# A decoder layer with routed experts: three shared-expert groups ahead of the routed blocks instead of four, and a new order around them

## What is computed

```
logits = xt @ gate_w.T + gate_b;  w, idx = top_k(sigmoid(logits), 2);  w = w / (sum(w) + 1e-08)
for e in range(6):
    h = silu(xt @ ew1[e].T) * (xt @ ew3[e].T);  y = y + ge[:, e:e+1] * (h @ ew2[e].T)
z = silu(xt @ fc1.T) * (xt @ fc2.T) @ fc3.T
out = x + y + z
```

## Time and profile before

| what | us |
|---|---|
| median of three runs | 1301.81 |
| lowest and highest run | 1296.87 and 1304.25 |
| the profiled execution's own time | 1303.18 |
| its span, first to last instruction | 1301.4 |
| its mean granted TensorE clock | 0.975 of 2.4 GHz |

### The profile page before, as it was taken

How to read it: one execution, slowest core, us unless ns; L and a number is a source line. 1 busy time by engine, 2 the same in 40 slices (tenths; PEclk the granted TensorE clock), 3 DMA queues, 4 the chain that set the end, 5 groups by cost and what they waited for, 6 DMA issues and landing times.

```text
span 1301.4 us, 34483 instructions
## 1 busy us (share of the span) xinstructions
PE 1210.7 (93%) x10882; PEld 1099.3 (84%) x10882; DVE 874.3 (67%) x2904; ACT 765.7 (59%) x1800; POOL 505.5 (39%) x709
## 2 busy tenths in 40 slices
PE   4899999999999779999999999999999888999984
PEld 4799899899998667989999999999998777888884
DVE  3765654755655557778778878888777675555548
ACT  3454443443544327788888888888887654555530
POOL 2341332431414342254444444444444531333335
PEclk9999999999999899999999999999999988999996
DMA  9499900000000335655566666655565243333359
GB/s 209 104 223 231 208 0 0 0 0 0 0 0 23 87 95 127 154 151 148 142 152 145 153 154 153 153 149 146 143 168 142 71 122 96 98 106 99 108 143 249
DMA packets 131263, 151.39 MB, mean 116 GB/s; under 512 B 41107, under 2 KB 111108, under 8 KB 131156
## 3 DMA queue, kind: packets, MB, share of 16 engines
q1 hardware_dynamic: 124436, 134.55, 42.5%
q0 software_dynamic: 6160, 15.69, 3.7%
q10 hardware_dynamic: 576, 0.07, 0.1%
HBM read 79.27 MB, written 45.82 MB: 96 GB/s over the span
## 4 chain that ended last, share of the span: by engine, by line
PE 51%; DVE 4%; issue 2%; POOL 2%; DMA 2%; ACT 1%; SPq 1%; DVEq 0%; POOLq 0%; ACTq 0%
PE psum L884 9%; PE psum L1135 7%; PE psum L1158 6%; PE psum L1172 6%; PE psum L1307 6%; PE psum L1327 3%; PE psum L1104 2%; PE psum L1153 2%; PE psum L1200 2%; PE psum L1186 1%; PE psum L1219 1%; DVE x_res L2356 1%; PE psum L1298 1%; PE psum L1315 1%; DVE x_res L2350 1%
## 5 line engine op out<-in xcount | busy, mean ns | idle before, releaser
L2219 DVE CUSTOM_DVE_ANT_0 junk<-psum,biasq 112x375 f32<-112x375 f32 x512 | 267.1, 542 | 95.0 <-issue 62.7
L1677 ACT ACTIVATE pr<-psum 125x448 f32<-125x448 f32 x384 | 204.3, 541 | 40.7 <-PE psum L1158 36.7
L1158 PE MATMUL psum<-qst,kst 97*125 97x224 f32 x768 | 192.8, 316 | 5.1 <-ACT psum L1686 5.0
L1135 PE MATMUL psum<-kst,qst 96*112 96x376 f32 x512 | 170.2, 356 | 4.0 <-DVE smax L2219 3.4
L1158 PEld LDWEIGHTS psum<-qst,kst 97*125 97x125 f32 x768 | 138.0, 189 | 17.6 <-ACT psum L1686 11.9
L1686 ACT ACTIVATE psum<-flagk 125x448 f32<-125x448 bf16 x240 | 131.7, 549 | 6.5 <-ACT pr L1677 0.4
L725 POOL TENSOR_TENSOR rs<-rs,neg_half 112x1 f32<-112x1 f32 x32 | 18.3, 571 | 243.3 <-DVE rs L2132 243.3
L850 POOL DMA_INDIRECT routed_y<-yb,yrow x61 | 58.9, 966 | 123.8 <-ACT yb L1868 118.1
L1135 PEld LDWEIGHTS psum<-kst,qst 96*112 96x112 f32 x512 | 89.6, 180 | 15.8 <-DVE smax L2219 5.9
L1172 PE MATMUL psum<-pr,vaug 125*32 125x112 f32 x3072 | 94.8, 264 | 0.0
L767 POOL DMA_INDIRECT routed_h<-h,slot x64 | 76.8, 1199 | 29.1 <-PE psum L1158 16.2
(11 more groups left out here) (321 smaller groups left out, 3501.8 us busy)
## 6 DMA issues: line engine op xcount, KB each, us to landing
kst<-khi SPq DMA_DIRECT2D x64, 376.0 KB, 4.9
routed_h<-in_route_pad SPq DMA_DIRECT2D x6, 3640.0 KB
kst<-klo SPq DMA_DIRECT2D x32, 376.0 KB, 6.3
ctxT<-in_ctxT SPq DMA_DIRECT2D x32, 375.0 KB
hblk<-routed_h SPq DMA_DIRECT2D x61, 130.0 KB
qst<-qhi SPq DMA_DIRECT2D x128, 56.0 KB, 2.5
stage<-in_e SPq DMA_DIRECT2D x21, 256.0 KB, 3.4
maskq<-in_mask SPq DMA_DIRECT2D x32, 164.1 KB
```

Source lines behind the costliest of these rows:

```text
L1135: pe.matmul(bank[max_bank(n, par, hd)][0:T, 0:S2E], head(qst[par][0:ROWS], hd), pair(kst[par][0:ROWS], hd // 2), start=True, stop=True).th ...
L1158: mm = pe.matmul(bank[q % 2][0:KP, cols(i, 2 * T)], pair(kst[par], n)[:, cols(q // HPB, KP)], both(qst[par], n), start=False, stop=True, s ...
L1677: nc.scalar.activation(pr[q % PROBS][:].rearrange("k i q -> k (i q)"), bank[q % 2][0:KP, 0:GT], ACT.Exp, scale=1.0 / HD ** 0.5).then_inc(s ...
L2219: nc.vector.tensor_tensor_reduce(out=junk[:, hd % 2, :], in0=bank[max_bank(n, par, hd)][0:T, 0:S2], in1=biasq[:, par, :], scale=1.0, scala ...
```

## The change

`FRONT` is 3: group 3 moves from the front to the tail. SyncE loads three groups between blocks 3 and 4 (4, 6 and 7, the latter two into buffers of their own, `h3last[0]` and `h3last[1]`) and group 5 behind the last block. The products have six buffers instead of four. In the front, VectorE does the slots of row 31 and `plan_blocks` earlier, and eight of the twelve low parts of weights instead of twelve; GpSimd does the last four, after its last scatter. GpSimd also issues the scatter of row 30 before it decides row 31.

```diff
-FRONT = 4
+FRONT = 3
+PRODUCTS = 6
+TURNED = (0, 1, 2, 3, 4, 6, 7, 5)
...
+        def raw_shared(g):
+
+            return h3last[g - (G - 2)][:] if g >= G - 2 else h3lo[g % 2][:].bitcast(F32)
+
+        def turned_at(g):
+
+            return 16 * DC * TURNED.index(g)
...
             def load_turned(g):
                 sp.wait_ge(s3["sent"], 16 * (GB * (g + 1) + 1))
-                if 2 <= g < G - 1:
+                if 2 <= g < G - 2:
                     sp.wait_ge(s["u_ps"], FC * G + DC * (g - 1))
                 if g >= 1:
-                    sp.wait_ge(s3["ht_in"], 16 * DC * g)
+                    sp.wait_ge(s3["ht_in"], turned_at(g))
...
             def load_products(g):
+                if g >= PRODUCTS:
+                    sp.wait_ge(s3["x_new"], added("routed", g - PRODUCTS))
                 if g >= RINGS:
-                    sp.wait_ge(s3["x_new"], added("routed", g - RINGS))
+                    sp.wait_ge(s3[f"first_in{g % RINGS}"], 16 * (g // RINGS))
...
                 if i == RINGS - 1:
                     load_turned(4)
-                    load_turned(5)
-            load_turned(6)
-            load_turned(7)
+                    load_turned(6)
+                    load_turned(7)
+            load_turned(5)
...
             scatter(*ahead(ROUNDS + 1, 1, -2))
-            landed(*ahead(ROUNDS + 1, 1, -2))
+            scatter(*ahead(ROUNDS + 1, 1, -1))
             decide(ROUNDS + 1, 1)
-            scatter(*ahead(ROUNDS + 1, 1, -1))
             landed(*ahead(ROUNDS + 1, 1, -1))
             scatter(ROUNDS + 1, 1)
+            for k in range(3 * (NE + 1) - STAGES, 3 * (NE + 1)):
+                low_expert(k)
...
             for i in range(NBLK):
                 scatter_block(i)
+            low_shared(5)
             low_shared(6)
             add_products(0)
-            add_products(1)
             low_shared(7)
-            for g in range(2, G):
+            for g in range(1, G):
                 add_products(g)
...
-                pe.wait_ge(s["w_lo"], PIECES + 3 + NE)
-                pe.wait_ge(s3["e13_lo"], 2 * NE)
+                pe.wait_ge(s["w_lo"], PIECES + 3 + NE + STAGES)
+                pe.wait_ge(s3["e13_lo"], 2 * NE - STAGES)
...
-            expand_shared(3)
             contract_shared(2)
-            contract_shared(3)
```

More of the change, by code:

```diff
@@ L291, in decoder_layer @@
             start = w3("start", [P, AHEAD])
-            h3last = w3("h3last", [P, DC, GT])
-            w3("gap", [P, GAP3 - DC * GT])
+            h3last = [w3(f"h3last{n}", [P, DC, GT]) for n in range(2)]
+            w3("gap", [P, GAP3 - 2 * DC * GT])
             e2 = [w3(f"e2_{part}", [P, NE, DC, D], F32R) for part in ("hi", "lo")]
             e13 += [w3("e13_lo", [P, NE, DC, 2, EW], F32R)]
-            products = [e13[n // 2][:].bitcast(F32).rearrange("p e c w n -> p (e c w n)")[0:T, n % 2 * GB * TOP * D:(n % 2 + 1) * GB * TOP * D].rearrange("t (j r d) -> t j r d", j=GB, r=TOP)
-                        for n in range(RINGS)]
+            products = [e13[n // 3][:].bitcast(F32).rearrange("p e c w n -> p (e c w n)")[0:T, n % 3 * GB * TOP * D:(n % 3 + 1) * GB * TOP * D].rearrange("t (j r d) -> t j r d", j=GB, r=TOP)
+                        for n in range(PRODUCTS)]
         apart = {nc.gpsimd.engine: sem("pool_waited"), nc.vector.engine: sem("dve_waited")}
@@ L364, in decoder_layer @@
         additions = [("shared", g) for g in range(FRONT)]
-        additions += [("shared", 4), ("routed", 0), ("shared", 5), ("routed", 1), ("routed", 2), ("routed", 3)]
-        additions += [("shared", 6), ("routed", 4), ("routed", 5), ("routed", 6), ("shared", 7), ("routed", 7)]
+        additions += [("shared", 3), ("shared", 4), ("routed", 0), ("routed", 1), ("shared", 5), ("routed", 2)]
+        additions += [("routed", 3), ("shared", 6), ("routed", 4), ("shared", 7), ("routed", 5), ("routed", 6), ("routed", 7)]
         def added(kind, g):
@@ L1833, in _ @@
             shared(1)
[L1834 to L1835 removed]
+            high_experts(2)
             shared(2)
[L1837 to L1839 removed]
+            high_experts(6)
             def high_block(i):
@@ L2355, in add_routed @@
                 dve.wait_ge(s3["x_new"], added("routed", g) - 1)
-                nc.vector.tensor_tensor(x[:, group(g), :], x[:, group(g), :], products[g % RINGS][:, :, 0], op=ALU.add).then_inc(s3["x_new"], 1)
+                nc.vector.tensor_tensor(x[:, group(g), :], x[:, group(g), :], products[g % PRODUCTS][:, :, 0], op=ALU.add).then_inc(s3["x_new"], 1)
             e13_pieces = iter(range(3 + NE, 3 * (NE + 1)))
@@ L2421, in _ @@
             shared(1)
+            slots(ROUNDS + 1, 1)
             add_shared(0)
+            plan_blocks()
             low_experts(2)
[L2424 to L2431, removed]
             add_shared(1)
-            low_experts(3)
-            shared(3)
+            shared(2)
             low_experts(2)
             add_shared(2)
-            add_shared(3)
             def low_block(i):
@@ L2481, in _ @@
             low_hidden_block(NBLK - 1)
+            shared(3)
             shared(4)
+            add_shared(3)
             shared(5)
@@ L2487, in _ @@
             shared(6)
+            add_routed(1)
             add_shared(5)
-            for g in (1, 2, 3):
-                add_routed(g)
[L2491 to L2496, removed]
+            add_routed(2)
+            shared(7)
+            add_routed(3)
+            add_shared(6)
+            add_routed(4)
+            add_shared(7)
+            for g in (5, 6, 7):
+                add_routed(g)
 def kernel(**inputs):
```

29 lines of the change are left out of this document (13 added, 16 removed).

## The result

The changed kernel takes 1305.18 us (median of 20 runs, 1300.33 to 1308.17) against 1301.68 for the kernel before (20 runs, 1296.04 to 1305.74), a ratio of 1.0026 with an interval of 1.0015 to 1.0036. It is a little slower, and less than 0.5% either way. Its profiled execution has a time of its own of 1306.32 us, a span of 1304.5 and a mean granted clock of 0.974. Before, these were 1303.18, 1301.4 and 0.975.

The account below looks back on a forecast made before the run. TensorE is busy 93% of the span, so only its waits in front and tail can give. Front +2.9 and tail -0.1 on 1303.18 give 1306.0, or 1304.6 us for the median, as that execution lay 1.4 above it; range 1296.5 to 1310.5.

Parts of the forecast that it names:

- Last weights' load: Front, SyncE: the load, released by VectorE's eighth low part, leaves at 1069.9, only 1.0 us earlier than before.
- Start of the blocks: End of the front, TensorE: blocks start at about 1077.5 instead of 1083.4, a gain of 6 us.
- Block 4: SyncE's third group load adds 4.3 us; block 4's load leaves at 1089.1, its transpose comes 0.6 us later than before.
- Idle time and clock: TensorE ahead of block 4: idles some 6 us, then the low clock costs +2.3 us (between 0 and 2.8).
- First routed addition: Tail, VectorE: the new group fills the idle 5.15 us and this addition starts 0.9 us later.
- The clash that the rival named: Tail: two `low_hidden` beside GpSimd cost up to 2.9 us more, delaying the first routed addition; the rival's chance 0.20.
- Behind it: Tail after the first routed addition: less stretching beside GpSimd, -1.4 us; three groups finished in a row, +0.4 us.
- Buffers: Tail: the two added product buffers, with product loads leaving 3.3 us earlier, count 0.
- the one with block 4 in time: Rival, front: SyncE's waits short or overlapped, so the front gives its whole 6 us: 1292.5 to 1295.8, chance 0.15.
- the new group would fall on the path: Rival, tail: the new group does not fit VectorE's idle gap; its whole 4.9 us gives 1309.5, chance 0.20.

Follow-up runs that it names:

- four groups in front: Kernel before with only the front's other edits (early slots and plan, GpSimd's four low parts, earlier row 30 scatter), `FRONT` still 4: 1303.06 us, ratio 1.0003.
- spread kernel: Changed kernel with only group 4 loaded between blocks 3 and 4, groups 6 and 7 before the loads of blocks 9 and 12: 1298.08 us, ratio 0.9975.
- sums of 8 columns: Changed kernel with GpSimd adding only 8 of the 256 columns of the products, so the output is wrong: 1298.69 us, ratio 0.9981.
- two groups in the gap: Changed kernel with groups 4 and 6 loaded between blocks 3 and 4, group 7 before block 12's load: 1300.51 us, ratio 0.9979.
- the same with spread loads: Kernel before with only the front's other edits, `FRONT` still 4, and group 5 loaded before block 5's load: 1302.72 us, ratio 1.0007.

## Why the prediction was right, and where its terms were off

The forecast was +2.8 us over the kernel before (1304.6 for 1301.8); the traces show +3.1, of which 0.5 lies ahead of P, and the medians +3.5. The steps one by one:

- **Last weights' load.** Predicted at 1069.9; it left at about 1070.35, which is the prediction plus the 0.5 by which this execution's front begins later. VectorE's list was read rightly.
- **Start of the blocks.** 1077.5 predicted, 1077.24 measured.
- **Block 4.** The place and the releaser are as forecast, and the experiment with the loads spread shows that this wait is the cause. Its size was off: I took 4.3 us for each further group in SyncE's list, and the steps from the first pair to the second and from the second to the third are 3.63 (1078.32 - 1074.69) and 3.43 (4.35 - 0.92). So the load left at 1088.34 and not at 1089.1, and block 4 came 0.6 earlier than before by the common point, not 0.6 later. The 4.3, worked out from the earlier trace rows, was one step of one execution, and I used it twice. With four groups in front and the same two loads the step was 3.51 (4.43 - 0.92, from 1076.06). The fit of the Trainium skill (DMA: Bandwidth & Descriptors, Anatomy of one DMA; it is for the GpSimd path) gives 2.5 us for 224 KB, and with the 0.92 of the two issues an estimate of 3.4 us a group; the measured 3.63 and 3.43 agree with it.
- **Idle time and clock.** 6 us of idle time predicted, 4.48 measured. Block 4 came 0.8 earlier than forecast (1090.52 for 1091.3), and TensorE reached the wait 1.0 later (1086.04 for 1085). The second is a term that I had wrong: the 7.3 us of work up to block 4 were read from the earlier trace rows, where the clock was up, and at the low clock of the changed kernel's first blocks they are 8.8. It cost nothing here, as the wait swallowed it; in the spread kernel it costs 1.5. The clock's price was 2.3, measured 2.7 between blocks 4 and 6 (7.85 against 5.17). Front: +2.9 predicted, +2.05 measured.
- **First routed addition.** Predicted 0.9 later, counted from the last block; it is 18.65 behind the first `hid` instead of 17.36, 1.3 later. The clash that the rival named is there: `low_hidden` took 2.49 beside GpSimd's first sum, 1.9 more than alone. But hardly any of it reached the path. With sums of 8 columns that `low_hidden` takes 0.62, and the first routed addition still comes 18.41 behind the first `hid`, since VectorE then waits 0.90 us for the contraction. The clash is worth 0.24.
- **Behind it.** The first routed addition itself is 0.9 longer, beside GpSimd's third low part (from 1267.84), which I had not priced. From its end to the last addition's end there are 29.0 us instead of 31.1, so -2.1, where I had -1.4. The end behind the last addition is 0.8 longer (4.5 for 3.7), not 0.4. Together +0.9 against the forecast -0.1.
- **Buffers.** Counted 0, worth 1.5. The -2.1 above holds this, so without the buffers it would be about -0.6 and not -1.4: GpSimd gets rid of its sums earlier and VectorE's last additions run alone. The step that failed is "As VectorE and not the DMA ends the tail, I count 0 for it". VectorE does end it, but its pace depends on when GpSimd's sums run, and that depends on the loads.

The terms of the front were 0.9 too high and that of the tail 1.0 too low (itself a sum of errors of both signs, the unpriced 0.9 one way and the buffers' 1.5 the other), and they cancelled, so the closeness of the total is partly luck. The mechanism, a gain eaten by the next load in SyncE's list and by the clock, is not.

Of the rivals, the one with block 4 in time gave 1295.8 for a kernel whose SyncE waits are short; the spread kernel, which makes them short, has 1298.1, as 5.0 of the 6 us reach block 4 and the tail is 1.0 longer than before (54.5 for 53.4). That the new group would fall on the path with 4.9 us didn't happen: 1.3 did.

## What to carry to other kernels

When an edit brings a stage forward, ask of every queue that feeds its next steps what now stands between them. A transfer that was hidden by 2.7 us of cover is the new bound once the stage starts 6 us sooner, and moving two loads a few blocks back is then worth more than the edit itself. A wait is not priced by its length alone. Here 0.8 us cost 0.8, and 4.5 us cost 7.2. An engine that "ends the stage" can still be made faster by moving the work of the engine beside it to another time. And a stretch of work that is read at the high clock is longer when idle time stands ahead of it: 8.8 us for 7.3 here.

## What the runs showed of the hardware

- TensorE's granted clock stayed at 1.00 (2.4 GHz) behind single idle times of 0.77 (block 4, two groups in the gap) and 1.55 us (block 20). It was at 0.50 (1.2 GHz) behind 2.70 (kernel before, 1070 to 1073), 3.47, 4.48 and 6.15. Several short ones in a row went both ways: 1.47, 1.06 and 0.80 ahead of the first blocks left it at 1.00 (four in front, 1083 to 1086), and 1.47, 1.09 and 0.80 were followed by 0.67 (the same with spread loads, 1078 to 1081). The price behind the 4.48, 2.7 us in two blocks, is near that of the 6.82 in the tail, 2.4 by the prediction's working: in these rows the longer idle time didn't cost more.
- VectorE and GpSimd take turns in the tail wherever both read SBUF, and each waits for the instruction of the other that is under way. Two rows of the kernel before, VectorE's `low_hidden` and the sum that GpSimd starts beside it:

```profile
1270.96 1.25 DVE L2332 TENSOR_TENSOR hid3lo<-hid,hid3hi 128x448 fp32r<-128x448 f32 x1 [0.63 <-ACT hid3hi L1806]
1271.70 2.76 POOL L855 TENSOR_TENSOR e_lo<-e_lo 112x1024 f32<-112x1024 f32 x1
```

  The sum ends at 1274.46, 2.25 behind `low_hidden`, about what a sum takes alone (2.34 to 2.41). In the changed kernel ten VectorE instructions with both inputs in SBUF start while GpSimd works. All six `low_hidden` end 0.48 behind the end of that GpSimd instruction (the one at 1263.30 ends at 1265.79, the sum at 1265.31), and all four routed additions 1.08 behind it (the first ends at 1271.05, the low part at 1269.96). The 1.58 us ones, too, are only the rest of a sum of 2.8 to 3.4 us in whose middle they start. `hid`, which has one input in PSUM, keeps its 0.6 beside GpSimd. The Trainium skill (SBUF — State Buffer, Who interferes with whom) has the second of such a pair fully blocked, and these rows agree; the prediction's reading, blocking by part of an instruction, saw instructions that begin in the middle of the neighbour. It is also why GpSimd, which VectorE hardly waits for by a semaphore, sets VectorE's pace.
- Reading 16 starting places on SyncE costs TensorE 1.5 us at each of two places in the blocks; in steps of 8 nothing of it is seen.
